# Pre-norm attention with a mixture of experts on eight cores: fewer side items per attention step, a third layer-norm buffer, and one engine for the first normalisations

## The reference

```python
x = x + attn(layernorm(x), W, b)              # x: (2, 8192, 1024), W: (1024, 3072)
x = x + moe(layernorm(x), router_w, w1, w2, shared_gate_up, shared_down, shared_gate_w)

def attn(x, W, b):
    q, k, v = split(x @ W + b, 3)
    logits = where(tril == 0, -9e15, (q @ k.T) / 32)
    return softmax(logits) @ v

def layernorm(x):                              # no scale, no shift
    return (x - mean(x)) / sqrt(var(x) + 1e-5)
```

## Time and profile before

| | |
|---|---|
| Median of 3 runs | 2621.6 us (2615.9 to 2827.58) |
| The profiled execution | 2619.8 us |
| Its span, slowest core (core 3) | 2617.8 us |
| Cores of that execution | 2599.4 to 2617.8 us |
| PE busy | 2157.1 us, 82% of the span |
| First QK of block 0, first shared-expert matmul | at 236.8 us and at 1457.5 us |

### The profile page before, as it was taken

How to read it: one execution, slowest core, us unless ns; L and a number is a source line. 1 busy time by engine, 2 the same in 40 slices (tenths; PEclk the granted TensorE clock), 3 DMA queues, 4 the chain that set the end, 5 groups by cost and what they waited for, 6 DMA issues and landing times.

```text
span 2617.8 us, 26288 instructions; the slowest of 8 cores (2599.4 to 2617.8 us)
## 1 busy us (share of the span) xinstructions
PE 2157.1 (82%) x9600; PEld 933.1 (36%) x9600; DVE 719.2 (27%) x933; ACT 722.8 (28%) x1268; POOL 58.7 (2%) x190
## 2 busy tenths in 40 slices
PE   1448899889699797879692465899999999999999
PEld 0113343334233243333240122344444444444444
DVE  3322332432523424243423111212031120302203
ACT  4313422422524424343423322110202112021120
POOL 0000000000000000000000000000000000000000
PEclk9768999999999999999796788899999999999999
DMA  7471420520513305151503232001131111221013
GB/s 153 100 121 39 95 37 29 115 61 6 116 47 61 74 25 115 37 98 45 107 25 83 40 56 49 0 1 33 34 64 33 33 33 33 52 45 33 1 33 129
DMA packets 204062, 149.70 MB, mean 57 GB/s; under 512 B 176160, under 2 KB 176288, under 8 KB 203936
## 3 DMA queue, kind: packets, MB, share of 16 engines
q1 hardware_dynamic: 189872, 101.88, 16.7%
q0 software_dynamic: 14064, 46.16, 9.9%
HBM read 142.79 MB, written 8.39 MB: 58 GB/s over the span
## 4 chain that ended last, share of the span: by engine, by line
PE 70%; DMA 9%; ACT 9%; ACTq 3%; DVE 3%; SPq 3%; issue 2%; DVEq 1%
PE pO L898 17%; PE sp L877 17%; PE pO L537 9%; PE pO L506 8%; PE pO L418 5%; DMA xb<-xq 3%; DMA xb<-xkv 3%; ACTq L51 3%; PE sp L349 3%; PE sp L797 3%; PE sp L802 3%; SPq L226 2%; PE pO L263 2%; PE pO L847 2%; DMA PTd<-P 2%
## 5 line engine op out<-in xcount | busy, mean ns | idle before, releaser
L877 PE MATMUL sp<-Q_sb,w 128*128 128x512 bf16 x2048 | 443.3, 379 | 0.0
L898 PE MATMUL pO<-w_sb,hb 128*128 128x512 bf16 x2048 | 443.3, 379 | 0.0
L418 PE MATMUL pO<-V_sb,PTd 128*128 128x512 bf16 x1088 | 285.8, 422 | 113.7 <-DMA PTd<-P 111.0
L907 DVE SCALAR_TENSOR_TENSOR O<-pO,c_sb,O 128x1024 f32<-128x1024 f32 x128 | 164.3, 1284 | 719.7 <-PE pO L898 719.7
L885 ACT ACTIVATE hb<-sp 128x1024 bf16<-128x1024 f32 x128 | 131.2, 1025 | 752.9 <-PE sp L877 752.9
L349 PE MATMUL sp<-K_sb,Q_sb 128*128 128x512 bf16 x1088 | 254.1, 389 | 60.3 <-ACT P L391 49.1
L877 PEld LDWEIGHTS sp<-Q_sb,w 128*128 128x128 bf16 x2048 | 200.4, 98 | 241.6
L898 PEld LDWEIGHTS pO<-w_sb,hb 128*128 128x128 bf16 x2048 | 200.4, 98 | 241.6
L506 PE MATMUL pO<-xlnT,wkv_sb 128*128 128x512 bf16 x1024 | 226.1, 383 | 50.0 <-DMA xlnT<-xlnb 50.0
L537 PE MATMUL pO<-wkv_sb,xlnT 128*128 128x512 bf16 x1024 | 232.1, 380 | 0.0
L418 PEld LDWEIGHTS pO<-V_sb,PTd 128*128 128x128 bf16 x1088 | 112.6, 106 | 281.5 <-issue 185.4
(11 more groups left out here) (81 smaller groups left out, 1042.4 us busy)
## 6 DMA issues: line engine op xcount, KB each, us to landing
xb<-xkv SPq DMA_DIRECT2D x64, 512.0 KB, 4.8
xb<-xq SPq DMA_DIRECT2D x32, 512.0 KB, 4.7
w<-w1p POOLq DMA_DIRECT2D x8, 2048.0 KB, 12.9
w_sb<-w2p POOLq DMA_DIRECT2D x8, 2048.0 KB, 12.9
out<-O SPq DMA_DIRECT2D x16, 512.0 KB, 2.6
wkv_sb<-wkvh POOLq DMA_DIRECT2D x2, 2048.0 KB, 29.2
wgu<-wguh POOLq DMA_DIRECT2D x16, 256.0 KB, 4.9
wq_sb<-wqh POOLq DMA_DIRECT2D x1, 2048.0 KB, 22.9
```

Source lines behind the costliest of these rows:

```text
L418: p.emit("tensor", lambda e, i=i, nb2_=nb2_, t=t, rr=rr, f=(i == 0), l=(i == nchunk - 1): e.matmul(pO[t % 2][:, nb2_ * 512:nb2_ * 512 + 51 ...
L877: p.emit("tensor", lambda e, e_i=e_i, th=th, fc=fc, dc=dc, nbq=nbq, jj=jj: e.matmul(sp[jj][:, nbq * 512:nbq * 512 + 512], w1_sb[e_i % 2][: ...
L898: p.emit("tensor", lambda e, th=th, tc=tc, fc=fc, nbq=nbq: e.matmul(pO[tc % 2][:, nbq * 512:nbq * 512 + 512], hb[th][:, fc * 1024 + tc * 1 ...
L907: p.emit("vector", lambda e, tl=tl, tc=tc, e_i=e_i: e.scalar_tensor_tensor(out=O[tl][:], in0=pO[tc % 2][:], scalar=c_sb[:, tl * 8 + e_i: t ...
```

## The change

Three edits. `xlnb` gets a third buffer and is taken in turn over three. In the opening every chain's normalised tile is written by DVE; the side items keep ACT (L213) for it. And the lower bound of `npop` goes from 4 to 3.

```diff
-    xlnb = [sba(f"xlnb{i}", [128, 1024], BF16) for i in range(2)]
+    xlnb = [sba(f"xlnb{i}", [128, 1024], BF16) for i in range(3)]
...
     def ln_back(key, src_fn, norm_eng="SC"):
-        xslot = ln_ctr[0] % 2
+        xslot = ln_ctr[0] % 3
...
-            ev_ln = ln_back(key, lambda xbs=xbs: xb[xbs][:],
-                            norm_eng="V" if (i - 1) % 2 == 0 else "SC")
+            ev_ln = ln_back(key, lambda xbs=xbs: xb[xbs][:], norm_eng="V")
...
-            npop = max(4, -(-kv_left // iters_left)) if iters_left > 0 else 4
+            npop = max(3, -(-kv_left // iters_left)) if iters_left > 0 else 3
```

## The result

| | before | after |
|---|---|---|
| Median of 10 runs | 2622.4 us | 2562.7 us |
| Ratio | | 0.9773, 95% interval 0.9761 to 0.9785 |
| Span of the profiled execution, slowest core (3 in both) | 2617.8 us | 2555.0 us |
| First shared-expert matmul, core 3 | at 1457.5 us | at 1394.1 us |

The change makes the kernel 59.7 us faster, against 61.7 forecast. All of it lies ahead of the shared expert, which core 3 starts 63.4 us earlier; its span is 62.8 us shorter. In some executions of every kernel the cores of one die run at a lower granted clock and take longer (up to 2858 us here), so ratios go by the other executions, and where a profiled execution is such a one, by the cores of the other die.

A forecast was written before the change was run, and what follows sets the result against it. PE was taken to wait on PTd<-P transposes held behind side items in SP's list. Gains of 73.7 us, less 3 (clock), 6 (late landings) and 3 (opening), make 61.7: from 2619.8 to 2558 us, range 2541 to 2592.

The forecast's parts named there:

- the recurrence: Attention blocks: with a load per step, an exponential ends 15.7 us after the one two steps earlier; PE needs 13.8.
- cost by the step: Rival, attention blocks: any load in a step stalls it, so spreading items adds 41 us, 2664 us in all; chance 0.05.
- Sum of the block terms: Attention blocks 0 to 7: three items a step gain 73.7 us, before 6 for late landings and 3 for the clock.
- late landings: Attention steps: transfers now closer together land later than their median, some 50 steps; 6 us off, between nothing and 20.
- Block 0, 10.0: Block 0, without p3: second to eighth QK takes 50.4 us by the chain instead of 60.4, a gain of 10.0.
- Blocks 1 and 4, 14.0 and 11.0: Block 1's tenth QK at 532.5 instead of 546.5, gain 14.0; block 4 some 69.4 us instead of 80.4, gain 11.0.
- Only the wait before QK(9) is over 3 us: Sign of being right, in block 1: the only PE wait over 3 us left is the 3.6 us stall there.
- Blocks 5 and 6, 3.0 and 2.5: Last group of each block loses its second p3; gain between nothing and 5 us of waiting, taken as 3.0 and 2.5.
- Block 7, 4.0: Block 7: the second l2t no longer stands ahead of the first PTd<-P, for which ACT waits 3.99 us; gain 4.0.
- The clock, 3 us lost: Blocks 1 to 3: the 3.6 us stall may let PE's clock fall, up to 2.7 us each, taken as 1 each.
- The opening, 3 us lost: Opening: DVE's late write sends chain 20's load into the weight load; K projection 3.0 us later, bounds gain 1, loss 7.8.
- by half only: Rival, attention blocks: late loads and transposes let stalls shrink by only half of 73.7, giving 2586 us; chance 0.20.

The follow-up runs named there:

- e9: The changed kernel with the lower bound of npop at 5 instead of 3: 2666.9 us, 1.0188 of the kernel before.
- e2: The kernel before with only the lower bound lowered to 3, two xlnb buffers and the opening as before: 2555.1 us, ratio 0.9741.
- e6: The changed kernel with the lower bound of npop at 2 instead of 3: 2522.1 us, 0.9636 of the kernel before.
- e7: The changed kernel with the two x loads for p3 issued early, ahead of the transposes of t5 and t6: 2541.8 us, 0.9708 of the kernel before.
- e4: The kernel before with 3 items instead of 4 in the last tile step of a block alone: 2609.2 us, ratio 0.9954.
- e1: The changed kernel with the opening as before, odd chains' tiles written by ACT: 2553.0 us, 0.9742 of the kernel before.
- e5: The changed kernel with the opening tiles of chains 9 and 17 written by ACT again: 2547.3 us, 0.9724 of the kernel before.
- e11: The changed kernel with lower bound 2 and the opening tiles of chains 9 and 17 written by ACT: 2513.2 us, 0.9592 of the kernel before.

## Why the prediction was right, and where its terms were off

The time was 2562.7 us against 2558.0, inside the range, and the mechanism holds: in block 1 SP's holds of 6 and 11 us are gone, what is left is the load on DVE in line with the softmax, and six exponentials come within 1 us of where the recurrence put them. e9 settles it against "cost by the step" and e2 shows that the bound does act and carries everything. But errors that cancel have a part in how close the sum came, and that part is luck: blocks 0 to 4 gave 52.7 us on the mean of five cores, where the terms less their 9 make 55.2, the opening lost 4.3 more than forecast, and the last three blocks gave 5.0 more.

- **Sum of the block terms, 73.7 less 6 for late landings and 3 for the clock, 64.7.** Measured 67.2 on the mean of five cores. Blocks 2 and 3 were 13.8 and 14.1 against 14.6 each, as worked out. PE's wait for PTd<-P was to fall to some 60 us and fell to 63.2.
- **Block 0, 10.0.** Core 3 gained 9.2, the mean only 5.2. The term came from one core, whose block 0 was 2.7 us longer before than the mean (192.6 against 189.9). This is a term read from too narrow a place. The steps were also miscounted: from the row of the second QK to the eighth the forecast took six steps of 6.9 us and got 50.4 with its stalls, and it became 52.9 on core 3. The row at the start holds two QKs with no AV between them. In block 1 of e6, where PE doesn't stand, it is 57.0 us from that row to the "tenth" QK, and not the 55.3 of eight steps; so block 1 lost 25.6 us to stalls before, and not 27.3, which also makes the step rival's price a little too high.
- **Blocks 1 and 4, 14.0 and 11.0.** 11.0 and 8.6 on the mean, 10.4 in block 1 on core 3. There 1.9 of the missing 3.6 us arise up to QK(10): a load of the key block, issued at 495.03, landed 5.9 us later instead of 4.8, and from then on the chain, counted from the block's start, ran a microsecond late and lost another by small steps. Another 1.3 are the wait ahead of the AV of 538.49, whose PTd<-P landed late behind an l2t. So the 6 us for late landings were the right kind of term, but they are landings behind another transfer of the same queue, not one in ten at random. The PTd<-P that landed 5.3 us after its issue, behind the load of p3, moved AV(6) by 3 us but not QK(9), which waited for the exponential longer still. The stall that e7 removes there is the one of 3.6 us that the forecast had counted. "Only the wait before QK(9) is over 3 us" was not met: in block 1 waits of 3.41 and 3.54 us stand near its two ends, as they did before. Block 4 was not followed.
- **Blocks 5 and 6, 3.0 and 2.5.** I took the middle between nothing and 5. Core 3 gained 6.3 and 7.0. The wait went nearly whole (4.2 and 3.8 us), so the middle was too low. And I had left out the clock: where the second wait goes, the AV behind it takes 3.6 us instead of 5.3 or 6.2, another 2.0 and 3.2. e4 shows that this one item is the cause.
- **Block 7, 4.0.** The wait shrank by 4.1 and 2.8 of it were lost to the clock. The step "everything to the end hangs on that" left out that PE had work in between before, and a 5.68 us hole now.
- **The clock, 3 us lost.** The term was for a clock that falls behind the stall before QK(9). In block 1 it didn't: the stall came in two parts, and QK and AV there take 3.61 us. Over the whole attention the clock gave: AV's matmuls got 21.5 us cheaper and QK's 2.6 dearer. In blocks 0 to 4 the distances in PE's timeline that I subtracted from already held this gain, so the sum missed it only behind them.
- **The opening, 3 us lost, range to 7.8.** It was 7.3 to 8.3, at the far bound; the full K projection was to start at 208 to 212 us and started at 215.3. The failed step: "the time from there to the full K projection grows by a square and the five small operations". It took for granted that chain 21's load would go out at 162 as before. But SP is held behind the transpose that follows, 18.65 us before and 20.07 now, and one load less gets out ahead of it. The row that would have told (163.44, on SP) stands right behind the one I quoted. e1 and e5 show that nothing else in the opening edit costs.
- **The third buffer, 0.** e1 against e2: 0.9742 and 0.9741.
- **Against the rivals.** The gain in blocks 1 to 3 was 38.9 us of 43.2, so "by half only" is out; e1, e2 and e9 put the rest out.

The rule of the Trainium skill that I weighed, "DMA: Bandwidth & Descriptors", section "Queues, rings and completion order", has each DMA engine take turns between queues, a packet at a time. I set it against the row of 25 us, and that was a mistake: the trace agrees with it, with 1080 packets of the one queue against 1012 of the other. What was wrong is what I made of it, a load at about twice its time. I counted neither the transpose that stands ahead of the load in the same queue nor its 1056 small packets, each of which lets one of 2 KB go by. So the rule and the row never spoke against each other.

## What to carry to other kernels

When background work is threaded into engines that run their lists in order, ask of every group what stands ahead of the critical transfer in each queue, and let no item wait for another item of its own group. A transfer is late by what stands ahead of it, so count the packets of that too, and not only the bytes. The number of items per step is worth sweeping: 5, 4, 3 (e2) and 2 (e11) gave ratios of 1.019, 1, 0.974 and 0.959 here (the first with the opening edit's some 0.003 in it), and the best value differed for the last block. Before a write is moved to another engine, look at what is queued there at the few places where it is urgent: two of twelve tiles made up the whole loss.

## What the runs showed of the hardware

- While two weight loads of 2 MB each were under way on POOL's queue (issued at 154.3 and 155.2, landed at 175.8 and 192.1 us before), the second DMA transpose on SP's queue took 18.65 us (before), 20.07 (after) to be issued, where 1.22 is usual, and everything behind it on SP waited. What holds the issue itself no run shows.
- The two queues took turns by the packet, whatever its size: 1080 packets and 2.18 MB against 1012 packets and 0.26 MB in 18 us. A transpose of 128x1024 bf16 is 1056 packets and took 24.3 us to land there, where 2.8 is the median.
- A PTd<-P issued right behind a 512 KB load on the same queue let AV go 5.5 us after its issue (515.71 to 521.25), and so did one in block 5 of the kernel before, issued at 1180.99 for the AV of 1186.49; the median of a landing is 2.8. The Trainium skill, "DMA: Bandwidth & Descriptors", section "Two DMAs through the same engine are not ordered", says that within one queue of an engine descriptors start in order. The rows agree: the transpose starts behind the load.
- After a wait of 5.68 us, 16 matmuls took 6.43 us, most of them at 1.2 GHz, and after one of 6.99 us 8 took 3.57 instead of 1.89; after one of 0.95 us 16 took 3.61, which is 2.4 GHz. Waits of one length can go either way: QK(3) of block 1 took 3.61 us behind 3.42 before and 5.30 behind 3.41 after. In all, the lower clock behind waits was 18.9 of the 69.9 us that PE gained in its two attention lines.
